# A two-layer transformer kernel: a third score pair may go into the two banks of the projection ring while an output group is open

## The reference

```python
xn = _layernorm(x)
x = x + attn0(xn) + ffn0(xn)        # layer 0: 8 key/value groups, each used by 4 heads; ffn width 1792, RMS norm in front
xn = _layernorm(x)
x = x + attn1(xn) + ffn1(xn)        # layer 1: 32 heads with their own keys and biases; ffn width 1376

# attn: scores = q k^T, masked above the diagonal, softmax(scores / sqrt(16)), times v, times Wo, plus bo
# ffn:  silu(xn Wg^T) * (xn Wu^T), times Wd^T
```

## Time and profile before

| | us |
|---|---|
| median of 3 executions | 831.46 |
| lowest, highest | 830.73, 834.44 |
| the profiled execution | 834.11 |
| its span, first to last instruction | 832.0 |
| PE busy in the span | 808.4 (97%) |
| DVE busy | 552.1 (66%) |
| ACT busy | 450.3 (54%) |
| POOL busy | 413.9 (50%) |
| waits of PE for other engines and DMAs, sum | 20.2 |
| mean granted clock of PE | 0.994 |

### The profile page before, as it was taken

The page is one execution under the profiler, slowest core; times in us unless marked ns, Lnnn a source line. Parts: engine busy times, 40 slices in busy tenths (PEclk is TensorE's granted clock), DMA queues, the critical chain, the costliest instruction groups (busy, mean ns, idle before and its releaser), DMA issues.

```text
span 832.0 us, 16422 instructions
## 1 busy us (share of the span) xinstructions
PE 808.4 (97%) x5596; PEld 625.4 (75%) x5596; DVE 552.1 (66%) x1576; ACT 450.3 (54%) x824; POOL 413.9 (50%) x551
## 2 busy tenths in 40 slices
PE   8999999998999999899999999998999999999997
PEld 4887776786976877676788876775677877767797
DVE  7877655588775578456687887555557767653455
ACT  3454554475655557355666665453556665545653
POOL 4544454446454455354544544448545545544541
PEclk9999999999999999999999999999999999999999
DMA  6657364633536364645667284847574386733341
GB/s 219 183 165 186 116 117 149 123 117 80 136 107 134 91 129 133 112 142 108 187 128 197 79 142 150 182 156 117 181 154 152 116 155 195 156 93 105 100 117 51
DMA packets 66321, 113.60 MB, mean 137 GB/s; under 512 B 13240, under 2 KB 16312, under 8 KB 66232
## 3 DMA queue, kind: packets, MB, share of 16 engines
q1 hardware_dynamic: 66240, 112.57, 54.3%
HBM read 87.57 MB, written 24.90 MB: 135 GB/s over the span
## 4 chain that ended last, share of the span: by engine, by line
PE 84%; DVE 8%; DMA 3%; issue 2%; POOL 1%; ACT 1%; SPq 1%; DVEq 0%; ACTq 0%; POOLq 0%
PE g_ring L1351 39%; PE acc L1351 24%; PE g_ring L1519 8%; PE s_bank L1498 3%; PE t_bank L1483 3%; PE t_bank L1498 2%; PE s_bank L1483 2%; PE acc L1483 1%; PE acc L1498 1%; DMA o_scratch<-o_t 1%; DMA q_op<-m_scratch 1%; POOL x L1072 1%; DVE x L1305 1%; DVE h L1227 1%; DVE xt_lo L1241 1%
## 5 line engine op out<-in xcount | busy, mean ns | idle before, releaser
L1060 POOL TENSOR_TENSOR w_lo<-w_raw,w_hi 128x512 fp32r<-128x512 f32 x204 | 271.8, 1336 | 169.9 <-ACT w_hi L1104 167.1
L1084 POOL TENSOR_SCALAR_AFFINE_SELECT p<-p 128x256 f32<-128x256 f32 (+1 forms) x320 | 119.5, 375 | 231.8 <-ACT p L1097 222.5
L1351 PE MATMUL g_ring<-xt_hi,w_hi 128*128 128x512 f32 (+1 forms) x504 | 207.4, 411 | 2.9 <-DVE qk_parts L1250 1.1
L1351 PE MATMUL g_ring<-xt_lo,w_hi 128*128 128x512 f32 (+1 forms) x504 | 197.7, 392 | 0.0
L1351 PE MATMUL g_ring<-xt_hi,w_lo 128*128 128x512 f32 (+1 forms) x504 | 197.3, 392 | 0.0
L1104 ACT ACTIVATE w_hi<-w_raw 128x512 fp32r<-128x512 f32 x204 | 127.9, 629 | 117.0 <-PE g_ring L1351 87.0
L1351 PE MATMUL acc<-w_hi,h_hi 128*128 128x256 f32 (+1 forms) x528 | 155.7, 295 | 4.7 <-DVE h_lo L1292 2.2
L1351 PE MATMUL acc<-w_lo,h_hi 128*128 128x256 f32 (+1 forms) x528 | 149.7, 284 | 0.0
L1351 PE MATMUL acc<-w_hi,h_lo 128*128 128x256 f32 (+1 forms) x528 | 149.5, 283 | 0.0
L1351 PEld LDWEIGHTS g_ring<-xt_hi,w_hi 128*128 128x128 f32 (+1 forms) x504 | 94.3, 187 | 38.7 <-issue 13.5
L1351 PEld LDWEIGHTS acc<-w_hi,h_hi 128*128 128x128 f32 (+1 forms) x528 | 101.2, 192 | 17.3 <-issue 11.0
(11 more groups left out here) (106 smaller groups left out, 1029.0 us busy)
## 6 DMA issues: line engine op xcount, KB each, us to landing
w_raw<-weights_in SPq DMA_DIRECT2D x204, 256.0 KB, 3.2
qk_scratch<-qk_parts SPq DMA_DIRECT2D x24, 512.0 KB, 3.5
q_op<-qk_scratch SPq DMA_DIRECT2D x96, 128.0 KB, 4.5
o_scratch<-o_t SPq DMA_DIRECT2D x32, 256.0 KB, 3.0
k_op<-qk_scratch SPq DMA_DIRECT2D x48, 128.0 KB, 7.3
context<-o_scratch SPq DMA_DIRECT2D x16, 256.0 KB
inverse<-r_scratch SPq DMA_DIRECT2D x16, 256.0 KB
k_op<-k_scratch SPq DMA_DIRECT2D x48, 64.0 KB, 5.1
```

The costliest lines, as they stand in the source:

```text
L1060: pool.tensor_tensor(w_lo[:, c % SPLIT, :], w_raw[:, c % RAW, :], w_hi[:, c % SPLIT, :].bitcast(F32), ALU.subtract).then_inc(split_done, 1)
L1084: pool.affine_select(out=view, in_=view, compare_op=ALU.is_ge, fill=0.0, base=0, pattern=[[0, n], [1, P]] if n == 2 else [[1, P]], channel ...
L1351: ins = pe.matmul(dst, w[a], xa[c], start=first and i == 0, stop=last and i == 2, skip_group_check=skip)
```

## The change

A fourth place is added, number 3: the two banks of `g_ring`. It is offered only while an output group is open (`state["open"]`), if more than `RING_LEFT = 2` steps of that group are still to come, and if no unit is waiting for its PV. It is free when the last two users of the ring are. A pair that takes it counts as two turns of the ring (`take("g")` twice); the next projection, norm tile or PV on that bank waits for that pair (`g_user`). `Mt` steps never use place 3. Waits for the ring now know three kinds of users: a pair, a PV, or anything else.

```diff
+RING_LEFT = 2
...
+        state["left"] = (KT if kind == "o" else FT[PHASES[ph][0]]) - 1 - tile
...
         if not state["open"]:
             a = state["acc"]
             times.append((max(freed("acc", a, 2), freed("acc", a + 1, 2)), 2))
+        elif state["left"] > RING_LEFT and held_pv(0) is None:
+            g = state["g"]
+            times.append((max(after("g", g - 2), after("g", g - 1)), 3))
         return sorted(times)
...
+            elif slot == 3:
+                a = take("g")
+                take("g")
...
-                end[("acc", a + job % 2) if slot == 2 else ("slot", slot)] = done
+                end[{2: ("acc", a + job % 2), 3: ("g", a + job % 2)}.get(slot, ("slot", slot))] = done
...
-        return max(at("smax", u), slots_by_time()[0][0])
+        return max(at("smax", u), min(x for x in slots_by_time() if x[1] < 3)[0])
...
+            if slot == 3:
+                return g_ring[a % 2], g_ring[(a + 1) % 2]
...
+                    if g - 2 in g_user:
+                        wait_pair(*g_user[g - 2])
+                    elif g - 2 in oev_of_g:
...
+                elif slot == 3:
+                    wait_g(a)
+                    wait_g(a + 1)
```

More of the change, by code:

```diff
@@ L150, in plan @@
     table = chunk_table()
-    state = {"t": 0.0, "chunk": 0, "g": 0, "acc": 0, "qk": 0, "hs": 0, "tj": 0, "gate": 0, "pv": 0, "open": False}
-    acc_user = {}
+    state = {"t": 0.0, "chunk": 0, "g": 0, "acc": 0, "qk": 0, "hs": 0, "tj": 0, "gate": 0, "pv": 0, "open": False, "left": 0}
+    acc_user, g_user = {}, {}
     end = {}
@@ L475, in visit @@
                 acc_user[a] = acc_user[a + 1] = (kind, p)
+            elif slot == 3:
+                g_user[a] = g_user[a + 1] = (kind, p)
         if placed:
@@ L502, in mtrans_ready @@
     def mtrans_ready(u):
-        return max(at("smax", u), slots_by_time()[0][0])
+        return max(at("smax", u), min(x for x in slots_by_time() if x[1] < 3)[0])
     def mtrans(u):
-        free, slot = slots_by_time()[0]
+        free, slot = min(x for x in slots_by_time() if x[1] < 3)
         a, before = -1, slot_user.get(slot)
@@ L668, in plan @@
             progress += cost
-    return {e: [s for _, _, s in sorted(x, key=lambda x: x[:2])] for e, x in line.items()}, acc_user
+    return {e: [s for _, _, s in sorted(x, key=lambda x: x[:2])] for e, x in line.items()}, acc_user, g_user
 def numbered(steps, *kinds):
@@ L687, in two_layers @@
 def two_layers(nc, x_in, weights, qk_bias, ln_w, bv, bo0, bo1, qk_scratch, k_scratch, m_scratch, o_scratch, r_scratch, out):
-    steps, acc_user = plan()
+    steps, acc_user, g_user = plan()
     PE, SE, VE, GP, SP = (steps[e] for e in ("pe", "act", "dve", "pool", "sp"))
```

17 lines of the change are left out of this document (8 added, 9 removed).

## The result

The changed kernel takes **836.49 us** (median of 12 runs, 833.29 to 839.92), the kernel before beside it on the same chip 832.37 (12 runs, 830.73 to 834.44). The ratio is 1.005, with a 95% interval of 1.0034 to 1.0066: slower by about 4.1 us where 1.0 faster was forecast, and 1.0 us beyond the upper end of the range. The profiled execution took 837.88 us, its span 835.7, at a mean granted clock of 0.992; the one of before had 834.11, 832.0 and 0.994. So the two profiles differ by 3.8 us, nearly what the medians do, and can be read against each other.

A forecast was written before the change was run, and what follows sets the result against it. PE was taken as the bound, busy 808 of 832 us. Fewer changeovers -1.0, old waits gone -8.9, new waits +7.5 and a clock fall +1.4 gave -1.0 us: 830.5 against a median of 831.46, range 826 to 835.5.

The forecast's parts named there:

- the signs of being wrong: PE's waits below 15 us, four or more clock falls between 170 and 320 us, or new waits in projection stretches.
- Part 1: Across PE's order: fewer visits and changes between dense work and visits or PV, -1.0 us (-0.6 to -1.3).
- Part 2: Old PE waits in re-ordered stretches disappear, -8.9 us in sum (-4 to -10).
- (b): Near 338.9 and 344.1 us: gate wait 0.97, unit 12's row wait 1.72 and slow PV 1.36 go, 4.05 us.
- (a): First open group, 170.6 to 205.7 us: waits at unit 6's `Mt`, a T pair and two output steps go, 2.9 us.
- (c): Near 427 us and between 600 and 700 us: waits go as stretches are ordered anew, 1.9 us.
- Part 3: New waits at back-to-back visits before PVs of units 4, 6, 10, unit 6's `Mt` and ring banks: +7.5 us.
- Part 4: One more fall of the clock, behind one of the two new 1.7 us waits: +1.4 us.
- B: Clock falls behind each of three back-to-back visits and the ring pair at unit 25's PV: 835.0 us, chance 0.13.
- A: New waits covered by h_lo waits, only +4 us of them and no further fall: centre 827 us, chance 0.22.
- C: Unit 12's rows still late because DMA engines are near full, 4.05 us stay: 834.5 us, chance 0.08.
- D: Extra place does little, waits move but add up the same: 830.5 to 831 us, chance 0.55 shared with the forecast.

The follow-up runs named there:

- experiment 5: Changed kernel with ring banks taken only when other places are used: 839.25 us; with ring allowed only in the last layer's down projection (six third pairs): 833.07 us.
- the queue edit: Kernel before, with the way back of unit 12's rows issued on SP ahead of the query loads: 831.29 us, ratio 0.9981.
- experiment 3: Changed kernel: maxima of units 6-8 shortened, 835.58 us (same on kernel before, 831.6); two maxima moved ahead of two h_lo on DVE, 835.97; that plus two fillers, 834.53.
- Experiment 4: Kernel before, planner told another duration: 0.70 for a maximum, 843.45 us; 0.68 for an h_lo, 836.95; 0.69 for a maximum (late rows only), 832.33.
- the last one: Kernel before, with unit 12's rows issued earlier on SP and idle matmuls ahead of the `Mt` of units 6 and 23: 829.16 us, ratio 0.9953.

## Why the prediction was wrong, step by step

**The signs I had set.** The sum of waits was forecast at 18 to 20 us and came to 23.2, against 19.5 before. Of the signs of being wrong two did not come: waits below 15 us, and four falls between 170 and 320 us (there were three). The third came: waits in the projection stretches, where I took the order to stay. The 1.56 us at 503 us is a projection, with no output group open; the new order had spread that far.

**Part 1** (-1.0 us) can't be read off alone. The 1.5 us by which the first two groups came out better than their waits and falls would fit it; the six third pairs of experiment 5 changed nothing measurable. It stays open, and no part of the miss needs it.

**Part 2.** (b) held in the trace: 0.97, 1.72 and the slow PV are gone. In the time it was worth less than its 4.05: the queue edit alone, which keeps the 0.97, shows 1.6 us. (a) held only in the sense that these waits were replaced. (c) failed: 1.9 us were to go "as those stretches are ordered anew". The 0.49 at 427 and the 0.54 at 659 went, the 0.59 at 678 became 0.17, but the 0.34 for rows at 689 became 1.44, and in the same stretches new waits came that no term held. The 1.29 us at 387.5, said to stay, went; the 0.60 at 617, which I had not named, stayed.

**Part 3.** The three back-to-back visits came as forecast, a little smaller: 1.60, 1.52 and 1.03 us for 1.7, 1.7 and 1.2 (at the PV of unit 4 the wait was for ACT's exponents, not for the maxima). The `Mt` of unit 6 was mis-sized: 3.08 us for 1.8. The row I took the earlier trace rows has DVE ready when PE ends the pair; here its list held two h_lo ahead, and experiment 3 showed that this makes the 1.3 us, most of it because the second took 1.76 us beside POOL's split. The upper bound had named a piece of DVE's list ahead of the maxima, the value taken had not, and that such a piece can take two and a half times its usual length stood nowhere. The waits on ring banks were put at 1.1 us; what came beside the four waits above was 1.56 (gate), 1.44 (rows by `m_scratch`), 0.78, 0.77, 0.56, 0.42, 0.41 and four of about 0.2, together 6.8. Of these only the 0.56 (at 403 us) and one of 0.22 (at 675) have a pair in the ring to do with them.

**Part 4.** One new fall was charged at 1.4 us; in the profiled execution there were two, at 1.4 and 1.7 by their PVs. The fall at 178 us came in three of the four profiled executions that have the bare wait of 1.6 us, the one at 228 in two of three, so on the average about 2.2 us of falls were to be charged.

The misses in the profiled execution, from the forecast's -1.0: +1.3 at the `Mt`, +1.7 for the second fall, 6.8 - 1.1 = +5.7 for waits in stretches ordered anew; -1.3 for the one at 387.5 and -1.1 for two of 0.53 at 491 and 500 us that went unforeseen, -0.5 for the visits back to back. Together +5.8, where 5.1 separate the forecast from the measured difference of the medians, and 4.7 from that of the profiles. **The step that failed** is the one behind (c) and the 1.1: I credited the old waits of every re-ordered stretch as gone and charged new ones only where I could see a visit behind a visit. A re-ordered stretch of this kernel has waits of its own: 6.8 us of them here, where the prediction had 1.1. Experiment 4 shows that this needs no third pair: two other orders without one are 4 and 10 us slower.

**The rivals.** B had the right size (835.0) and the wrong mechanism in half: falls behind two of its back-to-back visits, not behind all, and the rest of the loss elsewhere. A fell: nothing covered the new waits. C fell: the rows of unit 12 came in time, with the DMA share at 1.11 over those 4 us. D, "waits move but add up to the same", was right on the mechanism and wrong on "the same". The rule of the Trainium skill that I weighed (page "TensorE: Matmul & The Clock Gate", section "A second HAM failure mode: psum-queue depth-cycling") says that a PE that idles briefly and often between groups sees its clock swing between two levels. I had read it as every new wait bringing a fall, which is more than it says. The runs stand between: of the new waits of 1.0 to 1.6 us in the first 330 us, two of three brought one.

## What to carry to other kernels

When a change to a planner or scheduler re-orders whole stretches, do not price only the waits you can see: the waits of a new order are drawn again, and an order that was kept because it ran well has more to lose than to win (how this one was chosen no run here shows). Time one or two orders that differ for no reason (a constant moved by a few hundredths) beside the change, and take only what goes beyond their spread for the idea's own. If a single wait of the old order can be named, mend that one by hand and leave the rest: one DMA moved in a queue and fifteen idle matmuls gained 3.9 us here, the general rule lost 4.1.

## What the runs showed of the chip

- The same wait is followed by a fall of the clock in one execution and not in another. Behind the 1.85 us at the `Mt` of unit 23 it fell in nine profiled executions of the fifteen that have this wait; behind 1.64 to 1.68 us at the `Mt` of unit 6 in seven of eight; behind 1.52 to 1.78 us at the first T pair of unit 12 in three of seven. Behind the 1.29 us at 387 us it never fell, in ten; behind a wait of 1.03 us and one of 0.23 just after it, it did once (the kernel with the ring as last choice; the clock over 224 to 230 us was 0.72):

```profile
224.43 0.50 PE L1515 MATMUL s_bank<-q_op,k_op 50*128 50x512 f32 x2 [1.03 <-ACT p L1109]
225.16 0.79 PE L1500 MATMUL t_bank<-k_op,q_op 48*128 48x128 f32 x4 [0.23 <-DVE maxima L1330]
```

  So the length of one wait alone doesn't decide, and a forecast should charge a fall with a chance.
- With idle matmuls at a wait the clock stayed at 2.4 GHz in four profiled executions at two places each. Where their bank was free (178 us in the changed kernel, both places in the last one) they cost nothing that shows. Ahead of the `Mt` in the changed kernel their bank came free 2.5 us late, and the clock fell all the same. With no fall at all the mean clock was 1.000, the span 827.0 us.
- DVE and POOL slow one another. An h_lo (128x512, float32) that no POOL instruction overlaps takes 0.67 to 0.69 us, in all 43 cases of the two main traces; overlapped it takes up to 1.78, and all that took more than 0.9 were overlapped. The h_lo ahead of the `Mt` took 1.76 us in each of the five profiled executions that have it there.
- The first of three weight chunks that SP issued behind twelve operand loads was issued at 491.3 us, and ACT, which had waited 6.5 us for a chunk, split it at 500.4. The DMA engines were full from 488 to 500 us (share 0.99 to 1.11); PE, DVE, ACT and POOL all stood still for most of the 4.9 us. With such loads ahead of it a chunk has to be issued earlier.
